# Three-stage attention and FFN kernel: TensorE's order inside a unit, and its small pieces over 15 units

## The reference

```python
xn = layernorm(x)
q, k, v = layernorm_per_head(xn @ Wq + bq), ..., ...    # 16 heads of 8 features, with scale and bias
probs = softmax(q @ k.T * 8 ** -0.5)                    # per head, 512 x 512
x = x + (probs @ v) @ Wo + bo
h = silu(layernorm(x) @ w_gate.T) * (layernorm(x) @ w_up.T)   # 384 hidden features, dequantised weights
x = x + h @ w_down.T
```

## Time and profile before

| | us |
|---|---|
| median of 3 runs (424.13 to 425.54) | 424.87 |
| the profiled execution | 423.12 |
| its span, first to last instruction | 421.4 |
| TensorE busy in the span | 377.4 (90%) |
| ScalarE busy | 288.2 (68%) |
| VectorE busy | 240.7 (57%) |

### The profile page before, as it was taken

How to read it: one execution, slowest core, us unless ns; L and a number is a source line. 1 busy time by engine, 2 the same in 40 slices (tenths; PEclk the granted TensorE clock), 3 DMA queues, 4 the chain that set the end, 5 groups by cost and what they waited for, 6 DMA issues and landing times.

```text
span 421.4 us, 7237 instructions
## 1 busy us (share of the span) xinstructions
PE 377.4 (90%) x2383; PEld 154.7 (37%) x2383; DVE 240.7 (57%) x607; ACT 288.2 (68%) x322; POOL 47.4 (11%) x65
## 2 busy tenths in 40 slices
PE   4763899699999999899999999899989999999956
PEld 4533122043342533343343434253334434322445
DVE  4797108048935695459825893569645891244054
ACT  2301699587778787877787787868787777997601
POOL 6400002002002200201010200220020201020010
PEclk9756599899999999999999999999999999999989
DMA  3219504900456017600564036600760046500000
GB/s 106 63 47 199 81 0 157 167 5 1 151 103 125 2 60 177 130 10 0 177 126 70 0 114 135 124 0 16 200 129 2 0 150 128 98 2 0 27 1 25
DMA packets 32943, 32.74 MB, mean 78 GB/s; under 512 B 3608, under 2 KB 29848, under 8 KB 32920
## 3 DMA queue, kind: packets, MB, share of 16 engines
q1 hardware_dynamic: 32056, 32.19, 34.1%
q10 hardware_dynamic: 864, 0.26, 0.3%
HBM read 17.76 MB, written 14.68 MB: 77 GB/s over the span
## 4 chain that ended last, share of the span: by engine, by line
PE 60%; DVE 20%; DMA 5%; issue 5%; POOL 4%; ACT 3%; SPq 2%; DVEq 0%; POOLq 0%; ACTq 0%
PE oacc L703 19%; PE scores L689 12%; PE side L670 10%; PE side L614 5%; PE side L677 5%; DVE xn L865 4%; POOL rs L463 3%; DVE x2n L865 3%; PE side L630 3%; ACT probs L559 3%; DMA kst<-parts_dram 3%; PE side L661 2%; DVE stats L856 2%; DVE mv L859 1%; DMA parts_dram<-parts 1%
## 5 line engine op out<-in xcount | busy, mean ns | idle before, releaser
L559 ACT ACTIVATE probs<-scores 128x1024 f32<-128x1024 f32 x256 | 254.9, 1027 | 77.1 <-PE scores L689 74.7
L703 PE MATMUL oacc<-probs,vaug 128*32 128x512 f32 x1024 | 139.3, 617 | 0.5 <-ACT osb L533 0.4
L689 PE MATMUL scores<-qst,kst 50*128 50x512 bf16 x512 | 99.0, 396 | 16.4 <-DMA kst<-parts_dram 10.1
L689 PEld LDWEIGHTS scores<-qst,kst 50*128 50x128 bf16 x512 | 24.3, 93 | 166.3 <-issue 84.3
L461 POOL TENSOR_SCALAR ve<-mv 128x4 f32<-128x4 f32 (+1 forms) x17 | 4.0, 233 | 315.0 <-DVE mv L859 280.4
L703 PEld LDWEIGHTS oacc<-probs,vaug 128*32 128x32 f32 x1024 | 20.4, 109 | 32.6 <-issue 29.0
L1035 DVE TENSOR_TENSOR y<-side,x 128x512 f32<-128x512 f32 x7 | 4.8, 692 | 46.9 <-PE side L677 46.9
L670 PE MATMUL side<-x2T,wgT 128*128 128x512 f32 x42 | 22.7, 623 | 2.3 <-DVE x2T L1012 2.3
L865 DVE TENSOR_SCALAR xn<-x_in,mv,rs 128x128 f32<-128x128 f32 x32 | 17.4, 700 | 11.1 <-POOL rs L463 11.1
L670 PE MATMUL side<-x2T,wuT 128*128 128x512 f32 x42 | 22.9, 627 | 0.0
L677 PE MATMUL side<-wdT,hT 128*128 128x128 f32 x168 | 22.5, 284 | 0.0
(11 more groups left out here) (128 smaller groups left out, 371.3 us busy)
## 6 DMA issues: line engine op xcount, KB each, us to landing
parts_dram<-parts SPq DMA_DIRECT2D x24, 256.0 KB, 2.5
qst<-parts_dram SPq DMA_DIRECT2D x32, 192.0 KB, 4.9
kst<-parts_dram SPq DMA_DIRECT2D x32, 192.0 KB, 5.4
parts_dram<-parts SPq DMA_DIRECT2D x8, 384.0 KB, 2.6
parts_dram<-parts SPq DMA_DIRECT2D x24, 128.0 KB, 2.1
x_in<-in_L_attn_x SPq DMA_DIRECT2D x8, 256.0 KB, 3.5
x_res<-in_L_attn_x SPq DMA_DIRECT2D x8, 256.0 KB, 5.4
out_dram<-y SPq DMA_DIRECT2D x8, 256.0 KB, 2.0
```

Source lines behind the costliest of these rows:

```text
L559: act.activation(probs[:, kt, 2 * c:2 * c + 2, :], scores[:, 2 * c:2 * c + 2, :], ACT.Exp)\
L689: last = pe.matmul(scores[:, 2 * c + parity, :], kst[r, pair, kt * P:(kt + 1) * P], qst[r, pair, :], start=True, stop=True)
L703: last = pe.matmul(oacc[STRIP * j:STRIP * (j + 1), :], vaug[:, kt, NG * g + j, :], probs[:, kt, j, :], start=first, stop=last_of_half)
```

## The change

TensorE's order in a unit becomes: both score pairs, the unit's pieces, then the V product of unit u-1 (before: u-2, between the pairs). One V product is left behind turn 7 in place of two. The pieces stand in units 1 to 15: units 9 to 11, which had two each, now share with 12 and 13; d0 moves from unit 13 to 14 and d1 from 14 to 15. a_var is split into two halves, in units 5 and 6, in one bank as d0 and d1. The banks of u1, OT0 and the others follow. ScalarE copies `oacc` after both exponentials of units 0 and 8 (before: between those of 1 and 9), and the second and third tanh come after units 10 and 12.

```diff
--- before.py
+++ after.py
@@ -61,24 +61,26 @@
 
 
 
-SIDE = {1: ["a_xT"], 2: ["b_OT1", "a_q"], 3: ["b_onT", "a_k"], 4: ["b_Wo", "a_v"], 5: ["a_var"],
-        6: ["b_x2T"], 7: ["b_g0"], 8: ["a_rq", "a_rk"], 9: ["b_u0", "b_g1"], 10: ["b_u1", "c_OT0"],
-        11: ["b_g2", "b_u2"], 13: ["b_d0"], 14: ["b_d1"]}
-BANK = {"a_xT": 0, "b_OT1": 1, "a_q": 2, "b_onT": 0, "a_k": 1, "b_Wo": 2, "a_v": 0, "a_var": 1,
-        "b_x2T": 2, "b_g0": 0, "a_rq": 1, "a_rk": 2, "b_u0": 1, "b_g1": 2, "b_u1": 0, "c_OT0": 1, "b_g2": 2,
+SIDE = {1: ["a_xT"], 2: ["b_OT1", "a_q"], 3: ["b_onT", "a_k"], 4: ["b_Wo", "a_v"], 5: ["a_var0"],
+        6: ["a_var1", "b_x2T"], 7: ["b_g0"], 8: ["a_rq", "a_rk"], 9: ["b_u0"], 10: ["b_g1", "c_OT0"],
+        11: ["b_u1"], 12: ["b_g2"], 13: ["b_u2"], 14: ["b_d0"], 15: ["b_d1"]}
+BANK = {"a_xT": 0, "b_OT1": 1, "a_q": 2, "b_onT": 0, "a_k": 1, "b_Wo": 2, "a_v": 0, "a_var0": 1,
+        "b_x2T": 2, "b_g0": 0, "a_rq": 1, "a_rk": 2, "b_u0": 1, "b_g1": 2, "c_OT0": 0, "b_u1": 1, "b_g2": 2,
         "b_u2": 0, "b_d0": 1}
 
+SECOND_HALVES = {"a_var1": "a_var0", "b_d1": "b_d0"}
+
 LAST_SLOTS = {6: [], 7: ["b_x2T"], 8: ["b_g0"]}
-SIDE_ORDER = [p for u in range(NU) for p in SIDE.get(u, []) if p != "b_d1"]
+SIDE_ORDER = [p for u in range(NU) for p in SIDE.get(u, []) if p not in SECOND_HALVES]
 PHASE_PIECES = {
-    "before": ["a_xT", "a_v", "a_q", "a_k", "a_var", "a_rq", "a_rk"],
+    "before": ["a_xT", "a_v", "a_q", "a_k", "a_var0", "a_rq", "a_rk"],
     "first": [p for p in SIDE_ORDER if p[0] != "b"],
     "loop": SIDE_ORDER,
     "last": [p for p in SIDE_ORDER if p[0] != "a"],
 }
 
 
-EARLY = ["a_xT", "a_q", "a_k", "a_v", "a_var"]
+EARLY = ["a_xT", "a_q", "a_k", "a_v", "a_var0", "a_var1"]
 
 
 def sequence_of(piece, i):
@@ -303,7 +305,7 @@
         y_done = sem("y_done")
 
         read_out = {"xT": (xnT_done, 1, 0), "q": (qkc_done, 2, 0), "k": (qkc_done, 2, 1), "v": (vc_done, 1, 0),
-                    "var": (hv_done, 2, 0), "rq": (qkn_done, 2, 0), "rk": (qkn_done, 2, 1),
+                    "var0": (hv_done, 2, 0), "rq": (qkn_done, 2, 0), "rk": (qkn_done, 2, 1),
                     "onT": (onT_done, 1, 0), "Wo": (x2_done, 1, 0), "x2T": (x2T_done, 1, 0), "d0": (y_done, 1, 0)}
         read_out.update({f"OT{o}": (on_done, NO, o) for o in range(NO)})
         read_out.update({f"g{j}": (ga_done, NF, j) for j in range(NF)})
@@ -548,7 +550,7 @@
             act.activation(xnT[:, :], side[:, BANK["a_xT"], :], ACT.Copy).then_inc(xnT_done, 1)
             squares(1)
             SQUARES_AT = 4
-            TANH_AT = {"loop": {7: 0, 9: 1, 11: 2}, "last": {8: 0, 9: 1, 11: 2}}
+            TANH_AT = {"loop": {7: 0, 10: 1, 12: 2}, "last": {8: 0, 10: 1, 12: 2}}
 
             def turn(i, phase):
                 for u in range(NU):
@@ -558,10 +560,10 @@
                         act.wait_ge(qk_done, 2 * NU * i + 2 * u + c + 1)
                         act.activation(probs[:, kt, 2 * c:2 * c + 2, :], scores[:, 2 * c:2 * c + 2, :], ACT.Exp)\
                            .then_inc(exp_done, 1)
-                        if c == 0 and u == 1 and phase != "first":
-                            copy_o(i - 1, 1)
-                        if c == 0 and u == NU // NO + 1:
-                            copy_o(i, 0)
+                    if u == 0 and phase != "first":
+                        copy_o(i - 1, 1)
+                    if u == NU // NO:
+                        copy_o(i, 0)
                     if phase == "loop" and u == SQUARES_AT:
                         squares(i + 1)
                     if phase != "first" and u in TANH_AT[phase]:
@@ -617,10 +619,10 @@
             def piece(name, phase, i):
                 what = name[2:]
                 b = sequence_of(name, i)
-                if name != "b_d1":
+                if name in SECOND_HALVES:
+                    bank = side[:, BANK[SECOND_HALVES[name]], :]
+                else:
                     bank = bank_free(phase, i, name)
-                else:
-                    bank = side[:, BANK["b_d0"], :]
                 if what == "xT":
                     pe.wait_ge(xn_done, NT * (b + 1))
                     transposes(bank, lambda t: xn[:, t, :]).then_inc(xT_filled, 1)
@@ -635,14 +637,15 @@
                         last = pe.matmul(bank[:, t * D:(t + 1) * D], xnT[:, t * P:(t + 1) * P], wqkv[:, 2, :],
                                          start=True, stop=True)
                     last.then_inc(v_filled, 1)
-                elif what == "var":
-                    for w in range(2):
-                        pe.wait_ge(qksq_done, 2 * b + w + 1)
-                        for t in range(NT):
-                            o = (w * NT + t) * NH
-                            last = pe.matmul(bank[:, o:o + NH], qk_sq[:, w, t * P:(t + 1) * P],
-                                             group8[:, 0:P:HD], start=True, stop=True)
-                    last.then_inc(var_filled, 1)
+                elif what in ("var0", "var1"):
+                    w = int(what[3])
+                    pe.wait_ge(qksq_done, 2 * b + w + 1)
+                    for t in range(NT):
+                        o = (w * NT + t) * NH
+                        last = pe.matmul(bank[:, o:o + NH], qk_sq[:, w, t * P:(t + 1) * P],
+                                         group8[:, 0:P:HD], start=True, stop=True)
+                    if w == 1:
+                        last.then_inc(var_filled, 1)
                 elif what in ("rq", "rk"):
 
                     w = 0 if what == "rq" else 1
@@ -724,6 +727,8 @@
                 if name == "a_rq":
                     prepare_later_weights()
                 piece(name, "before", -1)
+                if name == "a_var0":
+                    piece("a_var1", "before", -1)
             for name in EARLY:
                 piece(name, "first", 0)
             pe.wait_ge(wT_copied, 3)
@@ -741,21 +746,20 @@
                     if u == NU // 2:
                         pe.wait_ge(stackB_loaded, 16 * STACK_DMAS * (i + 1))
                     slots = {**SIDE, **LAST_SLOTS} if phase == "last" else SIDE
-                    here = PHASE_PIECES[phase] + ([] if phase == "first" else ["b_d1"])
+                    here = PHASE_PIECES[phase] + [p for p, q in SECOND_HALVES.items() if q in PHASE_PIECES[phase]]
                     todo = [p for p in slots.get(u, []) if p in here and not (phase == "first" and p in EARLY)]
                     scores_of(i, u, 0)
-                    if u >= 2 or phase != "first":
-                        times_v(i, u - 2)
                     scores_of(i, u, 1)
                     for name in todo:
                         piece(name, phase, i)
+                    if u >= 1 or phase != "first":
+                        times_v(i, u - 1)
 
             turn(0, "first")
             turn(1, "loop")
             with pe.Fori(2, B - 1) as i:
                 turn(i, "loop")
             turn(B - 1, "last")
-            times_v(B, -2)
             times_v(B, -1)
 
             pe.wait_ge(y_done, B - 1)
@@ -896,7 +900,7 @@
                    .then_inc(vsum_done, 1)
                 dve.wait_ge(var_filled, b + 1)
                 dve.tensor_scalar(hv[:, 0:2, :, :].rearrange("p w t h -> p (w t h)"),
-                                  side[:, BANK["a_var"], 0:2 * NT * NH], HEAD_EPS, None, ALU.add)\
+                                  side[:, BANK["a_var0"], 0:2 * NT * NH], HEAD_EPS, None, ALU.add)\
                    .then_inc(hv_done, 1)
                 dve.wait_ge(vsum_done, b + 1)
                 dve.tensor_scalar(hv[:, 2, :, :].rearrange("p t h -> p (t h)"), v_sum[:, :], 1.0 / HD, HEAD_EPS,
```

## The result

The changed kernel takes 436.98 us (median; 435.52 to 439.81) against 424.50 us for the kernel before: the ratio is 1.030, with a 95% interval of 1.024 to 1.036. It is slower, and by more than forecast; the time lies outside the stated range of 421 to 433.

What follows compares the result with a forecast made beforehand. TensorE was taken to set the pace, held up by VectorE chains and an exponential. Ends -0.3 and -2.0, five turns of +0.95 (sum +2.5) and clock +1.5 took 424.9 to 428.9, rounded 429 us; range 421 to 433.

Steps and rivals of the forecast that it cites:

- TensorE's prices: Start-to-start costs on TensorE: two pairs 0.54 us to the next piece, V 1.00, lone weight product 1.03 with V behind.
- rival 1: V straight behind a full-array piece pays no 0.1 us gap: -6.6 to -7 us, 420.5 us in all; chance 0.20.
- rival 3: Hold as computed, no clock fall, half of the gap behind a piece hidden: 424 to 427 us; chance 0.12.
- d1 one unit later: From d1 to xT: chain stays 7.54 us, TensorE's work 4.61, so it is held 2.93 us, before 1.3.
- The rest of the turn: xT to Wo 8.12 us, Wo to g0 9.84, g0 to rq 2.57, rq to d1 18.95; turn 47.0, +0.95 each.
- The ends: Outside the five steady turns: -0.3 us in turn 0 and up to d1 of turn 1, -2.0 in the last turn.
- The clock: TensorE's clock halves after some of the five holds, 1.5 us each; one taken, +1.5 us, bounds 0 to 7.5.
- rival 2: Clock falls after most holds, three to five, adding 4.5 to 7.5 us: 432 to 435 us; chance 0.15.
- The sum: Whole kernel: -0.3 + 5 x 0.95 - 2.0 = +2.5 us, plus 1.5 for the clock, on the median 424.9.

Runs made afterwards that it cites:

- e1: Kernel after, with two f32 128x512 products on constants put into the hold ahead of a_xT in turns 2 to 6; 427.4 us, 1.0085 of the kernel before.
- e5: Kernel before with only the new order inside a unit; pieces, banks and tanh in their old places (d1 in unit 14); 422.4 us, 0.996 of the kernel before.
- e4: Kernel before, old order, with only d0 and d1 one unit later (units 14 and 15); 449.3 us, 1.057 of the kernel before.
- e2: Kernel after, with VectorE's statistics and xn of the next sequence put ahead of y; 418.6 us, 0.9875 of the kernel before.
- e3: Kernel before, with VectorE's statistics and xn of the next sequence put ahead of y; 422.8 us, 0.995 of the kernel before.
- e7: e1 with one f32 128x512 product in the hold instead of two; 431.15 us, 1.017 of the kernel before.
- e6: e2 with the pieces spread again (a_xT in unit 0, Wo and v alone, both var halves in unit 5); 407.2 us, 0.959 of the kernel before.

## Why the prediction was wrong

**TensorE's prices: right.** Two pairs take 0.53 or 0.54 up to the next piece. V behind a full-array piece starts 1.03 us (g0) and 1.06 us (u0) behind the piece's start; 1.03 was taken, 0.93 would have been rival 1. The turn without a fall is 47.16 us (e1) instead of 47.0, most of it between rq and d1. Rival 1 is out by those rows, and with it rival 3, which wanted half of the gap hidden. The Trainium skill's rule (TensorEngine Tiling (Array Packing), section Tiling Modes) that a change of tiling mode drains TensorE agrees with it: the V product behind a piece of its own type pays the gap. Whether the shape alone is the cause was not tried.

**d1 one unit later: right.** d1 to xT is 7.54 in before, after, e1 and e5 at the places shown, and 7.48 to 7.60 over all their turns; xn's chain starts at d1, and TensorE's own work in between shrank. The hold came as 0.50 at the exponential and 2.19 ahead of xT, 2.7 together, for 2.9; it was forecast in one piece, and came in two with a score pair between them. e4 shows it by itself, e2 by its absence.

**The rest of the turn: right.** Wo to g0 9.88 for 9.84, idle 0.76 for 0.7 to 0.8; g0 to rq 2.56 for 2.57; rq to d1 19.09 for 18.95.

**The ends: missed by 1.6 us, again by the clock.** The last part gave -1.8 for -2.0. Turn 0 and 1 came out at +1.1 for -0.3. The wait for the stack ended 36.06 us after the first score product instead of 36.92, 0.9 earlier for 0.4. But behind this wait, 2.16 us of idle time, the clock fell for longer than in the kernel before: from xT to d1 it took 42.22 us, where e1, with the clock at 1.00, takes 39.87 and 39.5 were computed. In e1 the ends give -1.6 and -0.8, -2.4 in sum for -2.3: the sum is right without the fall, and the split over the two ends is not.

**The clock: the step that failed.** The mechanism was named and its price per fall was right for a short one: a turn with it is 48.5 to 48.7, without 47.16, so 1.3 to 1.5 for 1.5. What failed is the count. I took one fall in five turns, with none and five as bounds, and put 0.45 on none to two and 0.15 on three to five. In the profiled execution there were five of five, and two of them lasted about twice as long and cost 2.8 and 2.6, which no term of the sum had: 245.62 - 5 x 47.16 = 9.8 us instead of 1.5. The two holds of the trace before, both followed by a fall, were the nearest rows to a hold of 2.9 us; the 0.6 us without a fall was much farther off. By the rule of the nearest row the count should have been all five, which gives 427.4 + 7.5 = 435, 2 us below the measured time; I had that as rival 2 at 432 to 435 and gave it too little. The range ended at 433 and so cut off most of a case that the nearest rows favoured. That rule would have been right here, but the runs don't make it a safe one: of four waits of 2.0 to 2.2 us at the end of turn 0, in this kernel and three of the experiments, only one was followed by a fall (last section).

**The sum, then:** 424.9 + 2.5 stands within 1 us (e1: 427.4, 3.3 us above the kernel before beside it); + 9.6 of clock, the measured distance from e1, instead of + 1.5 makes 437.0.

## What to carry to other kernels

When a piece of work moves later on an in-order engine, find the chain that starts at it and count what is left on the engine until that chain's end is needed: the hold is the difference, however small the move looks. A hold of some 2 us on TensorE can cost more than its length, when the products behind it run at half clock: here it did so five times of five with 0.50 us of idle time just ahead of it, and once of four without. Work that fills it, useful or not, was cheap (e1). And before spreading work, look whether the waiting consumer needs its producer at all: here xn hung on y by VectorE's program order alone, and moving it ahead turned +3.0% into -1.2%, and -4.1% with the pieces spread for both chains.

## What the runs showed of the hardware that was not expected

The granted clock fell after idle times on TensorE shorter than the two seen before (3.85 and 2.74 us). Idle times and falls in the nine profiled executions:

| Idle time of TensorE, us | Where | Clock fell to half |
|---|---|---|
| 3.47 to 3.90 | end of turn 0: before, e3, e4 | 3 of 3 |
| 2.70 to 2.81 | turns 2 to 6 of e4 | 5 of 5 |
| 2.73 to 2.74 | tail, all nine kernels | 9 of 9 |
| 2.62 | end of turn 0: e2 | 1 of 1 |
| 0.50, then 2.13 to 2.25 | turns 2 to 6 of the kernel after | 5 of 5 |
| 1.97 to 2.18 | end of turn 0: after, e1, e5, e7 | 1 of 4 |
| 0.50, then 1.08 to 1.20 | turns 2 to 6 of e7 | 1 of 5 |
| 1.02 | end of turn 0: e6 | 0 of 1 |
| 0.50, then 0.22 to 0.62 | turns 2 to 6 of before, e1, e5 | 0 of 15 |

Between the two idle times of one entry TensorE works 0.4 us (after) to about 2.4 us (e1).

The row of 1.97 to 2.18 is the surprising one. The kernel after and e7 have the same wait there within 0.02 us, and the same products in the same order; TensorE's row at the end of the wait and the table for 4 us behind it, first in the kernel after:

```profile
81.12 0.60 PE L692 MATMUL scores<-qst,kst 50*128 50x512 bf16 x4 [2.16 <-DMA kst<-parts_dram]
84.15:88.15 4.00, 4.00 (x19) 1.17 (x18) 1.09 (x3) 2.11 (x3) 0.00 (x0) 0.50 0.34 59
```

Then in e7:

```profile
80.24 0.60 PE L697 MATMUL scores<-qst,kst 50*128 50x512 bf16 x4 [2.18 <-DMA kst<-parts_dram]
83.24:87.24 4.00, 3.97 (x26) 1.41 (x28) 2.24 (x8) 3.69 (x4) 0.00 (x0) 1.00 0.39 71
```

The granted clock behind it is 0.50 in one and 1.00 in the other. So between about 1.1 and 2.2 us the length of the idle time alone does not tell whether the clock falls. What else decides is open.

A fall cost 1.3 to 1.5 us, or 2.6 to 2.8 where it lasted about twice as long, in the turns of the kernel after; what makes it long is open too. TensorE's clock in the first 50 us differs between the profiled executions of these kernels (its mean from 10 to 20 us is 0.57 in some and 1.00 in others), and the first score product stands at 42.9 to 45.6 us, with little changed ahead of it.
